# Second attention: q's inverse length as the scale of the exponential, with a bias from the unscaled maxima

## What is computed

```python
q = l2norm(q) * qs                    # l2norm(t) = t / max(|t|, 1e-12), per head
k = l2norm(k) * ksc
q, k = rotary_xpos(q, k)
# windows of 64 queries, each sees its own window of keys and the one before
sim = einsum('bhwid,bhwjd->bhwij', q * 8.0, look_around(k))
sim = where(mask, -finfo.max, sim)    # causal, at most 64 back
attn = softmax(sim, axis=-1)
out = einsum('bhwij,bhwjd->bhwid', attn, look_around(v))
```

## Time and profile before

| | |
|---|---|
| median of 3 runs | 1199.27 us (1199.17 to 1202.68) |
| the profiled execution | 1201.08 us |
| its span in the profile | 1199.3 us |
| instructions | 38346 |
| mean granted TensorE clock | 0.995 |

### The profile page before, as it was taken

One profiled execution on the slowest core, in us unless ns is written; L12 is line 12 of the kernel. 1 busy time (PEld: TensorE's weight loads), 2 busy tenths in 40 slices (PEclk: granted clock), 3 DMA queues, 4 the chain that ended last, 5 costly groups with the idle time before them and its releaser, 6 DMA issues.

```text
span 1199.3 us, 38346 instructions
## 1 busy us (share of the span) xinstructions
PE 1156.7 (96%) x14144; PEld 850.1 (71%) x14144; DVE 1033.7 (86%) x3938; ACT 990.8 (83%) x3034; POOL 969.4 (81%) x957
## 2 busy tenths in 40 slices
PE   8999999999999999999999999999999999999885
PEld 6677667777677766777677777777768777676664
DVE  6888898988988988897989899989999899979783
ACT  5888888898889889779888888897988979877772
POOL 2777786979887898787897988777897888989983
PEclk9999999999999999999999999999999999999998
DMA  6001010100101001010100100101000010001000
GB/s 220 19 11 26 19 30 4 27 20 22 31 17 27 7 22 36 16 26 21 22 22 21 26 19 15 30 13 26 21 21 17 14 28 16 21 19 30 22 18 22
DMA packets 31050, 31.32 MB, mean 26 GB/s; under 512 B 12560, under 2 KB 21392, under 8 KB 30736
## 3 DMA queue, kind: packets, MB, share of 16 engines
q1 hardware_dynamic: 30432, 28.08, 9.4%
q10 hardware_dynamic: 432, 0.79, 0.2%
HBM read 9.98 MB, written 2.10 MB: 10 GB/s over the span
## 4 chain that ended last, share of the span: by engine, by line
PE 85%; DVE 5%; ACT 5%; POOL 2%; issue 2%; DMA 0%; POOLq 0%; SPq 0%; DVEq 0%; ACTq 0%
PE psum L599 12%; PE psum L635 12%; PE psum L612 6%; PE psum L759 6%; PE psum L708 5%; PE psum L736 5%; PE psum L644 5%; PE psum L574 5%; PE psum L743 4%; PE psum L675 4%; PE psum L680 4%; PE psum L670 4%; PE psum L767 3%; PE psum L720 3%; PE psum L690 3%; PE psum L582 2%
## 5 line engine op out<-in xcount | busy, mean ns | idle before, releaser
L803 ACT ACTIVATE prob<-prob,negmax 128x512 f32<-128x512 f32 (+3 forms) x512 | 283.8, 558 | 16.8 <-DVE negmax L941 15.6
L941 DVE CUSTOM_DVE_ANT_0 prob<-psum,causal 128x512 f32<-128x512 f32 (+3 forms) x512 | 229.8, 482 | 10.1 <-PE psum L599 8.4
L1133 POOL TENSOR_SCALAR prob<-prob,rowinv 128x384 f32<-128x384 f32 (+1 forms) x256 | 160.7, 641 | 63.8 <-DVE rowinv L947 62.9
L858 ACT ACTIVATE b_prob<-b_prob,b_negmax 128x128 f32<-128x128 f32 x512 | 198.9, 394 | 3.3 <-DVE b_negmax L1014 3.2
L1153 POOL TENSOR_TENSOR r<-r 128x512 f32<-128x512 f32 x128 | 162.4, 1276 | 38.3 <-DVE r L980 38.1
L599 PE MATMUL psum<-k_t,q_t 64*128 64x384 f32 (+3 forms) x1024 | 179.1, 452 | 7.6 <-DVE u_t L1074 2.0
L635 PE MATMUL psum<-prob_t,v 128*64 128x256 f32 x1280 | 154.7, 383 | 0.2 <-DVE prob_t L953 0.2
L1014 DVE CUSTOM_DVE_ANT_0 b_prob<-psum,band,rnorm 128x128 f32<-128x128 f32 x512 | 146.2, 344 | 3.1 <-PE psum L708 2.9
L1183 POOL TENSOR_TENSOR b_prob<-b_prob,b_rowinv 128x1024 f32<-128x1024 f32 x64 | 121.7, 1901 | 16.6 <-DVE b_rowinv L1034 16.5
L612 PEld LDWEIGHTS psum<-ident,prob 64*128 64x128 f32 x2560 | 98.2, 138 | 39.5 <-issue 28.1
L1136 POOL TENSOR_TENSOR prob<-prob,rowinv 128x512 f32<-128x512 f32 x96 | 98.0, 1044 | 34.0 <-DVE rowinv L947 33.7
(11 more groups left out here) (101 smaller groups left out, 2840.4 us busy)
## 6 DMA issues: line engine op xcount, KB each, us to landing
vb_mid<-vb SPq DMA_DIRECT2D x112, 128.0 KB, 2.3
x_t<-in_x_t SPq DMA_DIRECT2D x8, 256.0 KB, 2.8
x_n<-in_x SPq DMA_DIRECT2D x8, 256.0 KB, 2.8
out<-x SPq DMA_DIRECT2D x16, 128.0 KB, 1.8
x<-x SPq DMA_DIRECT2D x64, 31.8 KB
wqkv<-in_wqkv SPq DMA_DIRECT2D x1, 1536.0 KB, 11.4
x<-x SPq DMA_DIRECT2D x48, 0.2 KB
w<-in_w SPq DMA_DIRECT2D x1, 682.0 KB, 13.2
```

Source lines behind the costliest of these rows:

```text
L803: last = af(pr, pr, ACT.Exp, bias=negmax[:, k % 4, o:o + 1], scale=-1.0, accum_out=rowsum[:, k % 4, o:o + 1])
L858: last = af(pr, pr, ACT.Exp, bias=b_negmax[:, a, o:o + 1], scale=-1.0, accum_out=b_rowsum[:, a, o:o + 1])
L941: vec.tensor_tensor_reduce(prob[:, k % PROBS, h, p * K:(p + 1) * K], bank[:, p * K:(p + 1) * K], causal[:, S - K:S], -E ** -0.5, 3.0e38, A ...
L1133: last = gp.tensor_scalar(pr, pr, rowinv[:, k % 4, h:h + 1], 1.0, ALU.mult, ALU.mult)
```

## The change

`b_max` takes the constant 1.0 as its factor and the maximum for the minimum; the k table loses its minus sign and the mask's sign turns, so the scores are no longer negated. `b_negmax` then holds the plain maximum, without q's inverse length, and the new step `b_bias` makes the bias of it: for each s one operation on 128x4, -1 times the maximum times q's inverse length. It waits for the four maxima and for `b_inverse_q`. `b_exp` waits for `b_bias` and reads q's inverse length as its scale.

```diff
@@ VectorE
-                dve.wait_ge(rnorm_q, nth("pool", "b_inverse_q", (l, n)))
                 bank = banks_of("b_scores", l, n)[s]
                 for c in range(CB):
                     o = s * CB + c
                     vec.tensor_tensor_reduce(b_prob[:, a, s, c, :], bank[:, c * P:(c + 1) * P], band[:, min(n % NT, 2 - n % 2), :],
-                                             rnorm[:, a, 0, 2 * c + s:2 * c + s + 1], 3.0e38, ALU.add, ALU.min, b_negmax[:, a, o:o + 1]).then_inc(b_max_ready, 1)
+                                             1.0, -3.0e38, ALU.add, ALU.max, b_negmax[:, a, o:o + 1]).then_inc(b_max_ready, 1)
+
+            def bias_b(l, n, s):
+                a, o = PLACE[l, n] % 2, s * CB
+                dve.wait_ge(rnorm_q, nth("pool", "b_inverse_q", (l, n)))
+                dve.wait_ge(b_max_ready, CB * nth("dve", "b_max", (l, n, s)))
+                vec.scalar_tensor_tensor(out=b_negmax[:, a, o:o + CB], in0=b_negmax[:, a, o:o + CB], scalar=-1.0,
+                                         in1=rnorm[:, a, 0, s::2], op0=ALU.mult, op1=ALU.mult).then_inc(b_bias_ready, 1)
@@ ScalarE
+                act.wait_ge(b_bias_ready, nth("dve", "b_bias", (l, n, s)))
                 for c in range(CB):
-                    act.wait_ge(b_max_ready, CB * (nth("dve", "b_max", (l, n, s)) - 1) + c + 1)
                     pr = b_prob[:, a, s, c, :]
                     o = s * CB + c
-                    last = af(pr, pr, ACT.Exp, bias=b_negmax[:, a, o:o + 1], scale=-1.0, accum_out=b_rowsum[:, a, o:o + 1])
+                    last = af(pr, pr, ACT.Exp, bias=b_negmax[:, a, o:o + 1], scale=rnorm[:, a, 0, 2 * c + s:2 * c + s + 1], accum_out=b_rowsum[:, a, o:o + 1])
```

```diff
-BANKS, LATE = 8, 14
+BANKS, LATE = 8, 15
+SINGLES, BY_ACT, BY_DVE = 0, 0, 0
...
-SWITCH, TABLES, SHY, PULL = {"128x128": 200, "64x128": 150, "128x64": 119, "64x64": 97}, 1283, 100, 0.01270
+SWITCH, TABLES, SHY, PULL = {"128x128": 202, "64x128": 155, "128x64": 150, "64x64": 97}, 1283, 180, 0.01853
-HURRY = {("act", "a_k"): 150, ("act", "a_q"): 750, ("act", "a_turn"): 150, ("act", "a_value"): 550, ("act", "b_exp"): -450,
...
+HURRY = {("act", "a_k"): -250, ("act", "a_q"): 700, ("act", "a_turn"): 50, ("act", "a_value"): 450, ("act", "b_exp"): -500,
...
+MARGIN = 50, 0
...
-            step("dve", "b_max", (*k, s), 1075, [("pe", "b_scores", k), ("pool", "b_inverse_q", k), before_2 and ("pe", "b_turn_p", before_2)])
-            step("act", "b_exp", (*k, s), 1555, [("dve", "b_max", (*k, s))], "exp")
+            step("dve", "b_max", (*k, s), 836, [("pe", "b_scores", k), ("dve", "tables", (LAYERS - 1,)), before_2 and ("pe", "b_turn_p", before_2)])
+            step("dve", "b_bias", (*k, s), 85, [("dve", "b_max", (*k, s)), ("pool", "b_inverse_q", k)])
+            step("act", "b_exp", (*k, s), 1555, [("dve", "b_bias", (*k, s))], "exp")
```

More of the change, by code:

```diff
@@ L43, with group_of, group_sequence, scaler @@
     HEADS_BEFORE[_u] = sum(2 * PAIRS_OF[x[1]] for x in UNITS[:UNIT[_u]])
[L46 to L53, removed]
+SIZE = [GROUP] * ((TILES - SINGLES) // GROUP) + [1] * SINGLES
+FIRST = [sum(SIZE[:g]) for g in range(len(SIZE))]
+GROUP_OF = {n: g for g in range(len(SIZE)) for n in range(FIRST[g], FIRST[g] + SIZE[g])}
+def group_of(n):
+    return GROUP_OF.get(n, -1)
+def group_sequence():
+    groups, behind = [], 0
+    for g in range(len(SIZE)):
+        groups.append((0, g))
+        if SIZE[g] < GROUP and g < len(SIZE) - 1:
+            continue
+        last = g if g == len(SIZE) - 1 else g - (2 if g >= LATE else 1)
         while behind <= last:
-            tiles += [(1, GROUP * behind + k) for k in range(GROUP)]
+            groups.append((1, behind))
             behind += 1
-    return tiles
-SEQUENCE = tile_sequence()
+    return groups
+GROUPS = group_sequence()
+SEQUENCE = [(l, n) for l, g in GROUPS for n in range(FIRST[g], FIRST[g] + SIZE[g])]
 PLACE = {k: i for i, k in enumerate(SEQUENCE)}
-def group_place(layer, g):
-    return PLACE[layer, GROUP * g] // GROUP
 def group_before(layer, g, back):
-    place = GROUP * (group_place(layer, g) - back)
-    return (SEQUENCE[place][0], SEQUENCE[place][1] // GROUP) if place >= 0 else (layer, -1)
+    place = GROUPS.index((layer, g)) - back
+    return GROUPS[place] if place >= 0 else (layer, -1)
+def scaler(l, n):
+    return "act" if PLACE.get((l, n), -1) >= len(SEQUENCE) - BY_ACT else "pool"
+def summer(l, n):
+    return "dve" if PLACE.get((l, n), -1) >= len(SEQUENCE) - BY_DVE else "pool"
 Step = namedtuple("Step", "engine name args ns after mode frees")
@@ L212, in make_plan @@
-            step("pe", "b_w2", g, 668 * GROUP, [("dve", "b_gate", (*g, CH - 1))], FULL, [[("dve", "b_w2", g)]])
-            step("dve", "b_w2", g, 341, [("pe", "b_w2", g)] + [("dve", "b_wo", (1, x)) for x in range(n - 3 * GROUP + 1, n - 2 * GROUP + 1)])
+                step("pe", "b_ffn", (*g, ch), 866 if z == GROUP else 456, [("act", "b_turn_f", g)], FULL, [[("dve", "b_gate", (*g, ch))]])
+                step("act", "b_gelu", (*g, ch), 0.833 * P * z + 160, [("pe", "b_ffn", (*g, ch)), ("pe", "b_w2", group_1)], "gelu")
@@ L296, in in_order @@
             left[x] -= 1
-            can[x] = max(can[x], done + LAG[s.engine][plan[x].engine])
+            can[x] = max(can[x], done + planned_lag(s.engine, plan[x].engine))
             if not left[x]:
@@ L301, in in_order @@
             to_empty[p, part] -= 1
-            emptied[p, part] = max(emptied.get((p, part), 0.0), done + LAG[s.engine]["pe"])
+            emptied[p, part] = max(emptied.get((p, part), 0.0), done + planned_lag(s.engine, "pe"))
             if not to_empty[p, part]:
@@ L764, in w2_mul @@
                 bank, = claim("b_w2", l, g)
-                for k in range(GROUP):
+                for k in range(SIZE[g]):
                     for ch in range(CH):
```

199 lines of the change are left out of this document (115 added, 84 removed).

## The result

The kernel got slower. The median of four runs is 1226.44 us (1225.13 to 1227.73), against 1200.5 us for the kernel before, measured beside it: a ratio of 1.0219, with a 95% interval of 1.0203 to 1.0235. The forecast was 1190 us with a range up to 1210, so both the direction and the range were wrong. The profiled execution took 1225.13 us, its span is 1223.3.

The account below looks back on a forecast made before the run. It took PE's own work and its order to bound the first stage, a dependent chain the last. Terms -7 - 3 - 1.6 + 2.4 + 0.5 - 0.5 = -9.2 us gave 1190 us; range 1178 to 1195, widened to 1210.

Parts of the forecast that it names:

- I price it at 0 on PE there: Before 1092 us, the exponentials' added ScalarE time was to cost PE nothing, since PE is served from queued work.
- The 47 us of the exponential: ScalarE work added by 512 exponentials reading their scale per row, at 92 ns each.
- PE's waits for ScalarE in the middle grow: A sign, named beforehand, that the prediction is wrong; no size was given.
- The 2.4 us that it was to cost in the last stage: After 1092 us, about 26 exponentials on the chain, each 92 ns longer: +2.4 us.
- The bias: On VectorE, 128 new small operations at 0.09 to 0.20 us each, 11.5 to 25.6 us in all.
- The order: Newly sorted queues: -7 us from fewer tile-shape changes (a quarter of them) and -3 us of PE idle time.
- the maxima: On VectorE, 512 maxima with a constant factor, 0.06 us less each: 30.7 us; 0.5 us back in the last stage.
- one wait for four: Exponential batches start after all four maxima and the bias: +0.5 us in the last stage, bounds 0 to +1.6.
- The 1.6 us for the later inverse length of q: Near the end, GpSimd computes it behind work that PE needs: 1.6 us off the chain.
- about 9: Sign expected: PE's idle time up to the end of the first attention stays about 9 us.
- ScalarE takes over: Rival, chance 0.17: exponentials longer than planned delay copies that free PSUM banks; 1207 us, or 1215 for a third.
- Less cover at the end: Rival, chance 0.13: with LATE 15 the last stage's chain has less work to hide it; up to 17 us, 1207 us.

Follow-up runs that it names:

- e3: Changed kernel with a constant exponential scale and the bias multiplied by ones, q's inverse length left out: 1206.32 us.
- e4: Kernel before, with only the second attention's exponential reading its scale (-1) per row: 1224.48 us.
- e8: Kernel before, with the exponential's scale read per row in layer 0 alone, 256 of 512 exponentials: 1215.96 us.
- e17: Kernel before, with the per-row scale on the first attention's 512 exponentials instead of the layers': 1215.66 us.
- e18: e13 with the exponential's scale (-1) read per row, in the old order: 1226.50 us.
- e16: Changed kernel's order with cheap maxima, constant scale and the bias step as a reduction, q's inverse length left out: 1200.67 us.
- e13: e5 with the bias step as a reduction over one element, in the old order: 1202.11 us.
- e1: Changed kernel's order and banks with the maxima, waits and exponential of the kernel before, no bias issued: 1206.24 us.
- e7: Kernel before, its maxima taking the constant 1.0, q's inverse length left out: 1202.11 us.
- e12: Kernel before, with the exponentials waiting once for all four maxima: 1202.61 us.
- e9: Changed kernel, planned anew with four exponentials at 1931 ns instead of 1555, due times kept: 1265.48 us.
- e10: Changed kernel planned anew with LATE back at 14: 1288.55 us.
- e11: Kernel before planned anew with LATE at 15: 1224.18 us.
- e5: e2 with a constant scale and a two-tensor bias multiplied by ones, q's inverse length left out, old order: 1215.40 us.
- e2: Kernel before in its old order, with the new maxima, bias, per-row scale and single wait: 1240.25 us.
- e15: Kernel before, with the second attention's exponential without a bias (maximum not subtracted): 1200.50 us.
- e6: e5 with the bias made by an operation with one tensor input: 1214.46 us.
- e14: Changed kernel with the bias as four 128x1 operations, each with a per-row scalar: 1233.11 us.

## Why the prediction was wrong

**The step that failed** is "I price it at 0 on PE there", with the reason "That is cover, though thin: PE is served from queued work". The 47 us of the exponential were seen rightly (488 ns measured, 486 forecast; ScalarE busy for 1032.5 us, 1038 forecast). What they cost was 0 + 2.4 us by the prediction, and 20 us (after less e3) to 23 us (e4) on the chip. The error was to take a mean, 881 of 1032 us busy, for slack in every stretch. Full stretches of ScalarE were there before, 11 windows of a hundred; they became 20. And PE's 9.1 us of idle time were taken for proof that no other engine counts, while its chain share fell from 85% to 65%. What the runs showed in place of the 0 is that PE is served late: its waits for ScalarE from 60 us to the last output matmul go from 0.3 to 5.5 us in the new order (e3 to after) and from 3.7 to 11.5 in the old one (before to e4). "PE's waits for ScalarE in the middle grow" was one of the prediction's own signs of being wrong. That the row scale alone does it is shown by e3, e4, e8, e17 and e18. The 2.4 us that it was to cost in the last stage came out as nothing in the new order (127.6 us left in e3, 127.5 after) and as 7.0 in the old one (129.5 before, 136.5 in e4). Open stays the part that PE's rows count as busy, 7.6 of 18.5 us between the profiled executions of e3 and after.

**The bias** was bounded at 0.09 to 0.20 us. The median of 165 ns is inside, the mean of 327 is not, since GpSimd held 36 of them. Its price of 5.6 us (e3 less e16) was missing, and with it VectorE's busy time came out 6.7 us higher instead of 5 to 20 lower. The earlier trace rows had no operation on two SBUF tensors, and I bounded the cost by a reduction, a form that e13 shows is not held. The trace of the kernel before does have such an operation, the last residual's sum, and its times (min/median/max ns) would have been the warning:

```profile
L1095 DVE TENSOR_TENSOR x<-x x16: 376/424/2537, 263.4 to 1193.0; 128x256 f32<-128x256 f32 x16
```

Without the hold the estimate was right: in e16 VectorE is busy for 1021.7 us, 12.0 less than before, and 12 was forecast.

**The order** was priced at -10 us. With the held bias and the row scale taken out it is worth 1.6 us: e16 has 1200.67 and e13, the same operations in the old order, 1202.11; the two intervals touch. The changes of tile shape did fall, though not by a quarter: from 60 to 1060 us I count 300 before and 274 after, in the stretch from 699.81 to 729.89 us 8 in both. 26 x 0.09 is 2.3 us, an estimate that takes the one measured pair of shapes for all; it is near what was measured. The order also moves 7 us between the stages: in e16 the last output matmul starts 7.1 us later than before (1076.9), and 7.6 us less are left behind it (121.9). But the order does serve the cheap maxima: with the old ones it has 1206.24 us (e1), while in the old order they are worth nothing (e7).

**Right** were the maxima (284 ns, 286 forecast) and one wait for four (+0.5 us forecast, e12 within the measurement). The 1.6 us for the later inverse length of q no run shows by itself. Two hits were luck. PE's idle time in the first stage came out near "about 9" (10.8 us), but in the new order it is 2.4 us without the row scale, which raises it to 9.9 (e3 and after, 60 to 1060 us). And the last stage did not get longer, 127.5 us for 129.5, because the order took 7.6 us out of it and the held bias put 5.7 back.

**Of the rivals**, "ScalarE takes over" had the mechanism and a chance of 0.17; it gave a sixth to a third of the 47 us, where the chip took 43 to 49%. Its explanation, the plan's wrong duration, is not borne out: the right duration made it worse (e9), though with due times that did not fit. "Less cover at the end" was half right: behind the last output matmul PE is idle for 28.0 us before and for 33.8 in e16 (38.3 after), but the stage has 13.4 us less of PE's work and gets shorter. `LATE` by itself could not be told apart (e10, e11).

**The sum as measured**: the order and the cheap maxima -1.6, the held bias +5.6, the row scale +20.1, together +24.1 us, of 25.9 found. These are the steps from the kernel before to e16, e3 and the changed kernel, so they have to add up; the 1.8 us that are left are the difference between the medians of the kernel before beside e16 (1202.24) and beside the changed kernel (1200.5). A test of the sum is in the old order: the bias costs 13.3 us (e5 less e13) and the row scale 24.4 (e18 less e13), 37.7 together, and e2, which has both, is 38.1 above e13.

**Open** stays whether a kernel with q's inverse length in the scale and a bias that is never held, in an order searched for the real durations, would do better. That was not tried. No version beats the kernel before by more than 2 us, and those that equal it (e7, e13, e15, e16) leave part of the work out, e12 apart.

## What to carry to other kernels

Where several engines are at 80% or more and the order is fixed, don't price added work at nothing because PE looks full: read the chain's share by engine and the count of full short windows. In this kernel 0.28 (e17) to 0.55 (e8) of ScalarE's added time was paid, which is a first estimate and no rule. Relief paid 0 to 1.7 us in an order made without it (e7, e15); the same cheaper maxima paid 5.6 us in the order that was planned with them (e1 less e16). So a change that moves time from one engine to another can pay for the load and get nothing for the relief. A tiny operation on SBUF beside a busy GpSimd can last 15 times its usual time (2641 ns for 170 in e5), and the same work in another form was never held (e13): look at the longest time of such operations too, and not at the median alone. A match between a forecast and a total can be two misses that cancel: compare with a run in the same order.

## What the runs showed of the hardware beyond that

- A VectorE operation on 128x4 elements lasted up to 2.64 us with two SBUF tensors and up to 2.66 with one (e5, e6), the long ones ending with a GpSimd operation. In the changed kernel it was held by GpSimd operations on 128x384 elements and more, and ran in its usual time inside the power on 128x8 (25 times). As a reduction it lasted 159 ns at most, and on 128x1 with a per-row scalar 216 (e13, e14).
- An exponential on 128x128 took 302 ns with a constant scale and no bias (e15), 394 with a bias read per row, 488 with the scale read per row as well (490 in e4): 92 to 96 ns for each.
- The fused maximum took 0.21 us of VectorE with a constant factor, in the changed kernel as in the earlier trace rows, and 0.27 with one read per row.
